# Score matmuls on 32 rows per head, and three phases that hold three sequences in flight

## The chip, the cores and the metric

The kernel runs on one core of a Trainium2 chip. The metric is the device time of one execution in microseconds, as the median of the runs. Names: TensorE (PE) multiplies matrices and loads weights (PEld), VectorE (DVE), ScalarE (ACT) and GpSimd (POOL) work on rows, SyncE (SP) issues most DMAs. SBUF is the on-chip memory, PSUM the eight banks that TensorE writes to.

## What is computed

Eight sequences (NB) of 512 rows (T) and 128 columns go through a layer norm, then three additions to the input: causal linear attention of 16 heads of 8 columns, sliding-window attention (64 rows back) and a gated FFN of 512 hidden columns with four layers. A second layer norm follows, then causal softmax attention and a mixture of 8 experts, of which each row takes 2.

```python
xn = layernorm(x)
h = rmsnorm(xn) * norm_w
q, k, v = h @ Wq, h @ Wk, h @ Wv
lin = causal(q_phi @ k_phi.T) @ v / sum          # q_phi, k_phi: 1, x, x*x/2 of q@Wqf, k@Wkf
win = softmax(window(q @ k.T) / sqrt(8)) @ v
x = x + xn + concat(lin, win) @ Wout + ffn(xn)   # silu(xn@w1)*(xn@w2) -> gelu(@h1) -> gelu(@h2) -> @w3
xn = layernorm(x)
x = x + softmax(causal(q2 @ k2.T) / sqrt(8)) @ v2 @ Wo + experts(xn)
```

## The kernel before

**Scores.** A head has 8 columns. For float32 accuracy q and k are split in a high and a low half, and a head has 32 rows (`ROWS`): three rows of 8 for halves, 8 for ones and for the row maximum that is subtracted. Four heads (`HG`) stand in the 128 rows of `Q1`, `QM`, `Q2` [128, G, 512]. The keys `K1`, `K2` are [128, 16, 512]: a head has 32 rows of its own and zeros in the other 96. So each score matmul takes all 128 rows, with the four heads' queries in them, and the zeros drop three of them (lines 515 to 580, the matmul is L549 in `scores_into`).

**Units and banks.** Work of TensorE is cut into units, each into one of 7 PSUM banks in turn. `UNITS` gives the order for each part of the program; each engine follows it by semaphores (`full` and `taken` of a bank). Units of a sequence: `lin` 40 (linear scores, keys times `QM`, ACT squares them), `cmax` 40 and `smax` 32 (scores with rows as output, of which DVE takes the maximum, L1279), `causal` 40 and `slide` 32 (ACT takes the exponential, L920), then projections, transposes (L528), FFN units (`gate`, `up`, `h1`, `h2`, `third_layer`), `mixed_first`, `mixed_causal`. In `lin`, `cmax` and `causal` five units are one pair of heads.

**After a pair** POOL masks it (`mask_tri`, `mask_slide`; L1079, L1082, L1092), DVE too for `slide` (`mask_middle`). After two pairs PE does `weigh` (L606), 32 matmul instructions of probabilities with V into the bank `heads`, four heads side by side in 32 columns of the array each; DVE or ACT copies the heads out, PE turns them (`rows`), DVE divides, PE turns back (`cols`). `probs` has four slots of a pair each; the FFN's hidden layers and the halves of q2 and k2 lie in the same memory, and the maxima's masked copies lie in `hT`, `xnT`, `hrow` and `spare`.

**Row maxima** go from `mx_c`/`mx_s` through a transpose (`turn_max`, L621), DVE's `negate_max` (L1304) and four DMAs of SP (`place_max`, L427) into a row of `Q2`/`Q1`, before `causal` or `slide` scores can start. **Halves** go through HBM: `split_and_send` (ACT makes the high half, DVE the low one, SP sends three times 256 KB), then `fetch` (four DMAs of 192 KB for keys, one of 1 MB for queries).

**Order.** One turn of the loop (line 1643 and its like) has four stages. *Linear*: `lin` of this sequence with `cmax` of the previous one, after `prefix` and the routing of rows. *Causal*: `causal` of the previous sequence with `smax` of this one. *Slide*: `slide` of this one, q, k and the gate/up layers of the next one. *Dense*: `h1`, `h2`, `third_layer` of the next one with `mix_first`, the second norm, q2, k2, v2 and `logits` of this one. An opening part does slide and dense for sequence 0, a tail part `cmax` and `causal` for sequence 7. Then 78 expert tiles follow (L845 to L861).

## Time and profile before

| what | value |
|---|---|
| median of 3 runs | 1597.93 us (1590.97 to 1603.12) |
| profiled execution | 1584.48 us |
| its span, first to last instruction | 1582.7 us |
| mean granted TensorE clock over the span | 0.917 |
| instructions | 28933 |

The profile is of one execution. Busy times of an engine are a union over its instructions, so that overlapping matmuls count once. A mean duration of a matmul holds its latency, and matmuls in a row start earlier than the one before ends. PEclk is the granted share of 2.4 GHz: 1.00 is 2.4, 0.50 is 1.2 GHz.

### The profile page before, as it was taken

Reading aid. Unit: us, or ns where it says so; the run is one execution under the profiler, and the core shown is the slowest. Engines: PE = TensorE matmul, PEld = TensorE weight load, DVE = VectorE, ACT = ScalarE, POOL = GpSimd, SP = SyncE. Lnnn points to the kernel's source line nnn. Section 1 sums busy time; section 2 is a strip of 40 time slices with the busy share of each in tenths; the row PEclk is TensorE's granted clock in tenths of the full one; section 3 lists DMA queues with packets and bytes.
Section 4 is the critical chain, followed back from the end, with each engine's and each line's share of the span. In section 5 each row is a group of like instructions: output and inputs, shape, how many; then the busy total and the mean of one; then the engine's idle time right before and its main releaser. Section 6 shows DMA issues by size and latency. Waiting matters only on the chain.

```text
span 1582.7 us, 28933 instructions
## 1 busy us (share of the span) xinstructions
PE 1363.4 (86%) x9122; PEld 933.8 (59%) x9122; DVE 823.8 (52%) x3372; ACT 708.2 (45%) x1503; POOL 601.5 (38%) x791
## 2 busy tenths in 40 slices
PE   5979878998899789988998899988997885679997
PEld 2555546655565556555656465556555664449997
DVE  3063375436653566347634764366536644826653
ACT  2345236523662356235643364236623640237765
POOL 6123233323341433233413342223414342618787
PEclk9989999997999899989998899979999995679999
DMA  9204400332022302240034004310233004204443
GB/s 264 60 2 113 108 16 7 96 86 62 7 75 65 104 9 68 54 119 10 30 93 114 14 4 120 84 40 7 75 87 82 7 8 149 85 18 62 62 63 48
DMA packets 82248, 102.09 MB, mean 65 GB/s; under 512 B 12473, under 2 KB 43105, under 8 KB 82017
## 3 DMA queue, kind: packets, MB, share of 16 engines
q1 hardware_dynamic: 63616, 86.53, 19.8%
q0 software_dynamic: 14304, 10.61, 4.3%
q10 hardware_dynamic: 4176, 3.01, 0.7%
q8 instruction: 85, 1.39, 0.4%
q14 instruction: 67, 0.54, 0.1%
HBM read 55.44 MB, written 46.37 MB: 64 GB/s over the span
## 4 chain that ended last, share of the span: by engine, by line
PE 62%; DVE 14%; issue 12%; ACT 5%; DMA 3%; POOL 2%; SPq 2%; DVEq 0%; POOLq 0%; ACTq 0%
PE bank L543 14%; PE bank L549 14%; PE heads L606 13%; PE bank L532 6%; PE bank L528 3%; PE bank L853 3%; PE bank L861 3%; DVE xnT_s L1279 2%; ACT probs L920 2%; DVE hrow L1279 2%; PE bank L647 2%; DVE hT_s L1279 2%; DVE mx_c L1279 1%; PE bank L537 1%; SPq L427 1%
## 5 line engine op out<-in xcount | busy, mean ns | idle before, releaser
L920 ACT ACTIVATE probs<-bank 128x512 f32<-128x512 f32 (+2 forms) x896 | 444.6, 578 | 489.4 <-PE bank L549 487.4
L549 PE MATMUL bank<-K,Q 128*128 128x192 f32 (+4 forms) x1024 | 243.9, 335 | 48.0 <-DVE attn L1320 13.7
L1079 POOL TENSOR_SCALAR_AFFINE_SELECT probs<-probs 128x384 f32<-128x384 f32 x256 | 127.7, 521 | 390.3 <-ACT probs L920 356.2
L606 PE MATMUL heads<-probs,V 128*9 128x192 f32 (+4 forms) x3072 | 225.4, 441 | 19.9 <-issue 14.3
L549 PE MATMUL bank<-Q,K 128*128 128x192 f32 (+4 forms) x1024 | 220.4, 329 | 25.3 <-DMA Q<-mrow_s 11.2
L549 PEld LDWEIGHTS bank<-K,Q 128*128 128x128 f32 x1024 | 181.5, 209 | 93.9 <-issue 30.6
L549 PEld LDWEIGHTS bank<-Q,K 128*128 128x128 f32 x1024 | 156.2, 201 | 59.0 <-issue 25.1
L549 PE MATMUL bank<-QM,K 128*128 128x512 f32 (+3 forms) x512 | 145.0, 379 | 44.7 <-DVE gatesT_s L1257 14.2
L606 PEld LDWEIGHTS heads<-probs,V 128*9 128x9 f32 x3072 | 81.0, 97 | 152.9 <-issue 120.0
L1141 POOL DMA_INDIRECT out<-h1T_s x78 | 124.0, 1589 | 54.0 <-ACT h1T_s L1033 27.6
L910 ACT ACTIVATE probs<-bank,sh_s 128x512 f32<-128x512 f32 x64 | 44.0, 687 | 207.9 <-PE bank L543 207.9
L549 PEld LDWEIGHTS bank<-QM,K 128*128 128x128 f32 x512 | 93.7, 219 | 67.1 <-DVE mx_c L1279 18.6
L543 PE MATMUL bank<-probs,h2T_s 128*128 128x512 f32 x256 | 114.2, 595 | 3.6 <-ACT probs L910 3.6
L1025 ACT ACTIVATE h2T_s<-bank,h1T_s 128x128 f32<-128x128 f32 x312 | 88.9, 368 | 62.7 <-PE bank L853 62.7
L543 PE MATMUL bank<-probs,h1T_s 128*128 128x512 f32 x256 | 115.2, 594 | 1.1 <-DVE probs L1447 1.1
L1092 POOL TENSOR_SCALAR_AFFINE_SELECT probs<-probs 128x512 f32<-128x512 f32 x64 | 56.0, 874 | 157.3 <-ACT probs L920 157.1
L1100 POOL TENSOR_TENSOR rs<-pw,half_neg 128x4 f32<-128x4 f32 x32 | 32.3, 1019 | 202.8 <-DVE pw L1241 202.8
L1308 DVE COPY ot<-heads 128x512 f32<-128x512 f32 x64 | 44.1, 690 | 106.0 <-PE heads L606 106.0
L1125 POOL DMA_INDIRECT sorted_rows<-rows,slot_i x64 | 63.4, 991 | 82.5 <-DVE rows L1376 63.9
L853 PE MATMUL bank<-h1T_s,w_in 128*128 128x128 f32 x624 | 84.2, 279 | 0.0
L861 PE MATMUL bank<-w_out,h2T_s 128*128 128x128 f32 x624 | 83.1, 276 | 0.3 <-ACT h2T_s L1025 0.3
L543 PEld LDWEIGHTS bank<-probs,h2T_s 128*128 128x128 f32 x256 | 47.4, 190 | 60.1 <-issue 56.6
(186 smaller groups left out, 2091.6 us busy)
## 6 DMA issues: line engine op xcount, KB each, us to landing
Q<-slots_of_q SPq DMA_DIRECT2D x16, 1024.0 KB, 10.6
K<-slots_of_k SPq DMA_DIRECT2D x64, 192.0 KB
QM<-slots_of_qm SPq DMA_DIRECT2D x8, 1024.0 KB, 8.7
slots_of_q<-Q SPq DMA_DIRECT2D x24, 256.0 KB, 3.0
slots_of_k<-QM SPq DMA_DIRECT2D x24, 256.0 KB, 4.0
slots_of_qm<-Q SPq DMA_DIRECT2D x24, 256.0 KB, 4.1
slots_of_q<-probs SPq DMA_DIRECT2D x24, 256.0 KB, 3.0
slots_of_k<-probs SPq DMA_DIRECT2D x24, 256.0 KB, 3.7
```

The lines of the kernel that those rows point to most:

```text
L532: pe.matmul(to_bank(run, unit)[:, :], w, x, start=True, stop=True).then_inc(full_sem(run, unit), 1)
L543: mm = pe.matmul(to[:, :], w[:, k, c * P:(c + 1) * P], src[k], start=(k == 0), stop=(k == FC - 1))
L549: mm = pe.matmul(to[:, at:at + right.shape[1]], left, right, start=True, stop=True, skip_group_check=True)
L606: mm = pe.matmul(heads[ROWS * i:ROWS * i + D + 1, P * j:P * j + widths[j]], V[:, j, HG * g + i, :], slot_of(kind, 2 * g + i // 2)[:, at:at ...
L853: mm = pe.matmul(tile_hidden_bank(i)[:, c * P:(c + 1) * P], w_in[:, i % WB, c * P:(c + 1) * P], tile_xT[:, i % 2, :], start=True, stop=True)
L861: mm = pe.matmul(tile_out_bank(i), tile_hidden[i % 2][:, c * P:(c + 1) * P], w_out[:, i % WB, c * P:(c + 1) * P], start=c == 0, stop=c == ...
L920: return act.activation(to, bank, func, scale=scale, bias=bias).then_inc(taken_sem(run, unit), 1)
L1025: last = act.activation(tile_hidden[i % 2][:, c * P:(c + 1) * P], tile_hidden_bank(i)[:, c * P:(c + 1) * P], ACT.Gelu, bias=tile_b1[:, i % ...
L1079: pool.affine_select(out=three, in_=three, compare_op=ALU.is_ge, fill=0.0, base=0, pattern=[[0, 3], [1, P]], channel_multiplier=-1)
L1125: pool.indirect_dma_start(out=sorted_rows, out_offset=bass.IndirectOffsetOnAxis(ap=slot_i[:, n:n + 1], axis=0), in_=rows[:, n // K2, n % K ...
L1141: pool.indirect_dma_start(out=out.rearrange("b t d -> (b t) d"), out_offset=bass.IndirectOffsetOnAxis(ap=tile_rows[:, i % XB, P + 1:P + 2] ...
L1279: last = dve.tensor_tensor_reduce(beside[:, at:at + n], bank_of(run, unit)[:, at:at + n], mask, 1.0, NEG, ALU.add, ALU.max, mx[:, to:to + 1])
```

## The change

- **Scores.** `K1` and `K2` become [128, G, 512], without zeros. `of_head` gives a matmul only the 32 rows of its head, of both operands. Pairs of heads are made new (`head_of`): the two heads of a pair have the same 32 rows, and units alternate between two pairs in neighbouring rows, so unit n and unit n + 1 are of different rows. Maxima (`other_rows`) are taken of the two row groups that the scores beside them don't use. The masks of two pairs come due together after ten units (eight for `slide`). The zeroing of the keys is gone.
- **Order.** Three phases take the place of four stages. *Window*: half of `cmax` (20 units) of the previous sequence with all `slide` of this one, then the norm, q, k, gate/up, `v1`, `h1_0` to `h1_2` of the next, `mixed_first`, second norm, q2, k2 of this. *Causal*: 8 `smax` of the next sequence (`WAKE`) with `h1_3` and `logits`, then `causal` of the previous with the other `smax`, `prefix` and the routing of this. *Linear*: `lin` of the next sequence, with `h2`, `third_layer`, the rest of `causal`'s heads, `v2`, and in its second half the first 20 `cmax` of this (`EARLY`). Opening, first, last and tail are the same three phases with parts left out.
- **Buffers.** `hidden` (two sets of four FFN layers), `halves` (six of 512 columns) and `masked` (seven) are buffers of their own; `dens`/`rdens` are one for each group.
- **Weights.** `wout` and `wo1` are loaded in the new order of heads, by 16 DMAs of ACT instead of two.

The core of the diff (what is the same thing again on another engine is left out):

```diff
-LEAD, BEHIND = 12, 8
+PAIRS, TRI, WINDOW = H // 2, 40, 32
+GROUP, WGROUP = TRI // G, WINDOW // G
+def head_of(pair, half):
+    return 8 * (pair // 4) + 4 * half + pair % 4
+def tri_of(n):
+    return 2 * (n // GROUP) + n % 2, n % GROUP // 2
+def other_rows(n, group):
+    return (n // group ^ 1) * group + n % group
+EARLY = 20
+WAKE = 8
+def slide_by(n):
+    return min(WINDOW, 4 * (n + 1 - EARLY))
+WINDOW_WEIGH, WINDOW_TURN = {24: 0, 26: 1, 28: 2, 30: 3}, {26: 0, 28: 1, 30: 2, 32: 3}
+GATE = {27: 0, 28: 1, 29: 2, 30: 3}
+HIDDEN1 = {31: 0, 34: 1, 36: 2}
+CAUSAL_WEIGH, CAUSAL_TURN = {16: 0, 26: 1, 36: 2}, {22: 0, 32: 1}
+LIN_WEIGH, LIN_TURN = {16: 0, 26: 1, 36: 2}, {22: 0, 32: 1}
+HIDDEN2 = {0: 0, 6: 1, 12: 2, 19: 3}
...
-            Q1, QM, K1 = sb("Q1", [P, G, T], F32R, early), sb("QM", [P, G, T], F32R, early), sb("K1", [P, H, T], F32R, early)
+            Q1, QM, K1 = (sb(n, [P, G, T], F32R, early) for n in ("Q1", "QM", "K1"))
+            hidden = sb("hidden", [P, 2, FC, T], F32, early)
+            halves = sb("halves", [P, 6, T], F32R, early)
...
             def body(run, before, this, after):
                 part, b = run
-                if before and this:
-                    place_max(run, "causal_max", mrow_c, Q2, "placed_c")
-                if this:
-                    place_max(run, "slide_max", mrow_s, Q1, "placed_s")
                 if after:
                     for name in ("q1", "k1", "qm1"):
                         split_and_send(run, (b, 1), name)
...
+                    for name in ("k1", "q1", "qm1"):
+                        fetch_sent((b, 1), name)
+                if this:
+                    for name in ("q2", "k2"):
+                        split_and_send(run, (b, 0), name)
+                if before:
+                    place_max(run, "causal_max", mrow_c, Q2, "placed_c")
+                if after:
+                    place_max(run, "slide_max", mrow_s, Q1, "placed_s")
+                if this:
+                    if before:
+                        sp.wait_ge(taken_sem(run, CAUSAL_UNITS[-1]), taken_at(run, CAUSAL_UNITS[-1]))
+                        sp.sem_inc(S["unread"], 1)
+                    for name in ("k2", "q2"):
+                        fetch_sent((b, 0), name)
+                if before:
                     store(run, b - 1)
...
-            def q_part(buf, h, a, n):
-                return buf[:, h // HG, a:a + n]
+            def of_head(buf, h, a, n):
+                i = h % HG
+                return buf[ROWS * i:ROWS * (i + 1), h // HG, a:a + n]
...
+            def window_phase(run, before, this, after):
+                _, b = run
+                now, nxt = (b, 0), (b, 1)
+                if this:
+                    turn_heads(run, now, LIN, 2)
+                    pe.wait_ge(S["placed_s"], due("placed_s", now, PLACED))
+                s = 0
+                for n in range(EARLY, TRI):
                     if before:
                         causal_max(run, n)
+                    while this and s < slide_by(n):
+                        slide_scores(run, s)
                         s += 1
...
+            def causal_phase(run, before, this, after):
...
+                for n in range(WAKE):
+                    if after:
+                        slide_max(run, n)
+                    if n == 1 and before:
+                        turn_max(run, "causal_max", mx_c, CMAX_UNITS[-1])
+                    if n == 2 and this:
+                        wait_taken(run, "xnT2")
+                        project_rows(run, "logits", xnT, wgT[:, :], E)
+                    if n == 3 and after:
+                        dense(run, "h1_3", h1T, hidden_a, 3)
+                if before:
+                    pe.wait_ge(S["placed_c"], due("placed_c", previous, PLACED))
...
+            def linear_phase(run, before, this, after):
...
+                if after:
+                    pe.wait_ge(S["slots_qm1"], due("slots_qm1", nxt, 16))
+                for n in range(TRI):
+                    if after:
+                        tri_scores(run, LIN_UNITS, K1, QM, n)
+                    if n == TRI - EARLY and this:
+                        pe.wait_ge(S["slots_k2"], due("slots_k2", now, PLACED))
+                        pe.wait_ge(S["slots_q2"], due("slots_q2", now, 16))
+                    if n >= TRI - EARLY and this:
+                        causal_max(run, n - TRI + EARLY)
...
+            for g in range(G):
+                for half in range(2):
+                    row, first = ROWS * g + 2 * D * half, D * head_of(2 * g, half)
+                    act.dma_start(wout[row:row + 2 * D, :, :], dram["wout"].rearrange("a p n -> p a n")[first:first + 2 * D]).then_inc(S["mix_weights"], 16)
+                    act.dma_start(wo1[row:row + 2 * D, :], dram["wo1"][first:first + 2 * D, :]).then_inc(S["mix_weights"], 16)
...
-            pool.memset(K1[:, H // 2:H, :].bitcast(F32), 0.0).then_inc(S["keys1_cleared"], 1)
```

## Rows read from the trace of the kernel before

**Rows 1.** The page, part 1: busy us, share, instructions

```profile
PE 1363.4 (86%) x9122; PEld 933.8 (59%) x9122; DVE 823.8 (52%) x3372; ACT 708.2 (45%) x1503; POOL 601.5 (38%) x791
```

**Rows 2.** Windows: length, busy of PE, PEld, DVE, ACT, POOL, PEclk, DMA share, GB/s

```profile
17.00:67.30 50.30, 46.05 (x135) 22.49 (x133) 7.38 (x15) 14.55 (x19) 20.12 (x32) 1.00 0.56 155
67.30:187.10 119.80, 103.75 (x671) 68.09 (x670) 50.80 (x217) 52.46 (x99) 32.01 (x47) 0.91 0.18 52
187.10:1191.70 1004.60, 894.08 (x5854) 577.29 (x5852) 543.08 (x2280) 452.38 (x839) 331.56 (x494) 0.93 0.22 60
1191.70:1327.00 135.30, 107.74 (x831) 75.29 (x831) 76.84 (x349) 58.15 (x116) 46.84 (x79) 0.87 0.11 30
1327.00:1413.00 86.00, 57.45 (x307) 38.46 (x307) 43.96 (x180) 21.30 (x41) 40.67 (x52) 0.71 0.33 98
```

**Rows 3.** The same for the four stages of one turn, and their sum

```profile
519.80:577.50 57.70, 44.41 (x257) 28.65 (x258) 37.02 (x178) 21.73 (x39) 20.27 (x32) 0.85 0.21 56
577.50:612.00 34.50, 30.07 (x271) 21.45 (x269) 23.29 (x140) 24.32 (x46) 13.94 (x28) 1.00 0.02 5
612.00:644.80 32.80, 31.55 (x259) 21.02 (x260) 16.62 (x31) 19.25 (x41) 12.49 (x18) 0.95 0.29 89
644.80:687.30 42.50, 41.56 (x193) 23.62 (x192) 13.17 (x35) 9.62 (x15) 8.04 (x6) 1.00 0.32 84
sum 167.50, PE 147.60 PEld 94.74 DVE 90.10 ACT 74.91 POOL 54.75; mean PE 36.90 PEld 23.69 DVE 22.52 ACT 18.73 POOL 13.69
```

**Rows 4.** Chain of waits, 500 to 720 us: start, us, what

```profile
586.49 3.79 PE bank L549 x25
590.27 0.45 PE bank L528 x4
...
600.59 2.27 PE heads L606 x32
...
624.20 6.89 PE bank L532 x16
...
632.37 0.41 PE bank L628 x2
...
644.86 3.48 PE bank L543 x8
...
652.21 1.31 PE heads L606 x32
...
666.40 1.78 PE bank L638 x16
...
676.50 1.98 PE bank L532 x4
...
683.60 3.69 PE bank L647 x32
```

**Rows 5.** Row maxima by window (L1279), and the page's group of ScalarE

```profile
577.50:612.00 34.50, 15.44 (x108) 1.00 0.02 5
...
sum 167.50, DVE 45.21; mean DVE 11.30
...
L920 ACT ACTIVATE probs<-bank 128x512 f32<-128x512 f32 (+2 forms) x896 | 444.6, 578 | 489.4 <-PE bank L549 487.4
```

**Rows 6.** Busy time by window, where TensorE does maxima alone

```profile
1359.00:1365.60 6.60, 6.60 (x16) 4.07 (x16) 6.60 (x33) 0.00 (x0) 5.08 (x6) 0.50 0.19 62
```

**Rows 7.** Groups of TensorE by shape: xcount, busy us, mean ns

```profile
L606 PE MATMUL heads<-probs,V 128*9 128x512 f32 x512 | 79.0, 694 | 5.3 <-POOL probs L1082 5.2
```

**Rows 8.** Chain of waits: placing the maxima, and keys in the tail

```profile
606.95 0.29 DVE mrow_s L1304
...
612.00 0.92 PE bank L549 x6
...
1330.79 6.39 DMA K<-slots_of_k
```

**Rows 9.** Timeline of ScalarE's queue, one of 21 loads

```profile
12.31 0.60 ACTq L1044 DMA_DIRECT2D b_s<-in_b  x1
```

## What I expect of the change, and why

> **What bounds the kernel now.** I read the page's shares first. No engine is full: TensorE is busy 86% of the span, VectorE 52%, ScalarE 45%, GpSimd 38% [rows 1]. Next, the span cut by sequence: set-up, an opening, the first sequence, six turns of the loop in 1004.6 us (167.4 each), the last, a tail, and 169.7 us of expert tiles after 1413 [rows 2]. The loop is two thirds of the time, so one turn matters most. Cut into its four stages [rows 3] it shows four limits. The dense stage (42.5 us) is matmul: TensorE 41.56 busy, ScalarE 9.62, VectorE 13.17. The linear stage (57.7 us) is nobody's: TensorE 44.41 at a mean clock of 0.85, VectorE 37.02. PE and DVE take turns, each running dry while the other has a block. Causal (34.5) is mixed, slide (32.8) is TensorE again.
>
> I then priced TensorE's work by the chain of waits, at full clock [rows 4]: a score matmul 3.79 / 25 = 0.152 us; a `weigh` block of LIN or CAUSAL 2.27, of SLIDE 1.31; four transposes 0.45; a 512-column projection 6.89 / 8 = 0.86; one hidden unit of the FFN 3.48; `mix_first` 1.78; `v` or `logits`, as wide as a projection or the same number of instructions, 0.85; a pair of `mix_causal` or `prefix` instructions 0.41; `third_layer` 3.69. A sequence has 320 score matmuls.
>
> **The change, part by part.** Nothing of the arithmetic goes away; three things change.
>
> *(1) Order.* The four stages become three phases, each with dense work between scores. TensorE's work at today's prices:
>
> - Window: 32 + 64 score matmuls 14.6; `weigh` 2.27 + 4 x 1.31 = 7.5; 12 turns 5.4; 13 projections 11.2; `v1` 0.85; three hidden units 10.4; `mix_first` 1.8. Sum 51.8.
> - Causal: 128 scores 19.5; 3 `weigh` 6.8; 2 turns 0.9; two `turn_max` 0.7 (an estimate, under two sets of four transposes, 0.9); `prefix` 5 x 0.41 = 2.0; `logits` 0.85; one hidden unit 3.5. Sum 34.3.
> - Linear: 96 scores 14.6; 4 `weigh` 9.1; 6 turns 2.7; `v2` 0.85; `mix_causal` 8 x 0.41 = 3.3; four hidden units 13.9; `third_layer` 3.7. Sum 48.1.
>
> Together 134.2 of 167.4 us. VectorE's 90.1 us [rows 3] split so: the maxima are 45.2 in all [rows 5]. The second row there is 108 records, four to a `slide_max` unit, so 27 units at 0.57; that leaves 26.5 for 40 causal maxima, 0.66 each. Window gets 20 causal maxima (13.2) and most of the copies, splits and gates, about 37; Causal 32 slide maxima (18.3) and the routing, about 28; Linear 13.2 and about 12 more, 25. The split of the rest is my estimate. ScalarE makes a probability unit in 444.6 / 896 = 0.50 us [rows 5]: 40 in Causal 20 us, 40 in Linear 20 us, 32 shorter ones in Window. It is nowhere the largest. GpSimd has 54.75 us a turn [rows 3]; by my count of masks, powers and row DMAs no phase gets over about 23. So Window and Linear are TensorE's, Causal is between VectorE and TensorE.
>
> *(2) Scores on 32 rows, neighbours in other rows.* Today K is 128 rows with zeros for the other heads, so matmuls follow one another. Afterwards unit n and n+1 use different row groups and banks. Before has no row-tiled matmul. The nearest row is `weigh`, whose four column tiles do run at once: 512 instructions of 694 ns mean are a union of 79.0 us, 154 ns each [rows 7]. Bounds: nothing saved (0.152 stays), or all four at once (a quarter, 48.6 to 12.2 us a sequence). Both parts of a unit use the same rows and bank and must follow one another; only the next unit can start beside the second part. I take a half: minus 7.3, 9.7, 7.3 us.
>
> *(3) Changes of array shape.* Scores on 32-row tiles alternate with 128x128 and with the 32-column `weigh`. Today only the 12 `weigh` blocks change the shape, 24 changes; I count 93 after (39, 20, 34). Price: a hidden unit is 3.48 for 8 instructions of 512 columns, 0.435 each; a LIN `weigh` is 8 steps side by side with 2 x 1280 columns, 2.18; it takes 2.27 [rows 4]. So a change costs up to 0.1 us; nothing excludes 0 below, and above, its whole latency, about the 0.3 us by which a 694 ns `weigh` matmul outlasts its column time [rows 7]. I take 0.1: plus 2.9, 1.4, 2.6. The Trainium skill, TensorEngine Tiling (Array Packing), Key Properties, says that changing the tiling mode drains the engine. That speaks against this change; it gives no price, and by the rows the drain is small.
>
> TensorE afterwards: 47.4, 26.0, 43.4.
>
> *Waits.* Window: from `mix_first` done (666.40 + 1.78 = 668.18) to the q2 projection (676.50) is 8.3 us of VectorE, GpSimd and ScalarE [rows 4]. Covered today by h2 units; afterwards by `h1_2` 3.5, four maxima units and two turns, some 5.6, so 2.7 shows. The phase begins on masks of the last linear pair, `up3` must be gated before `h1_0`, rows before cols: 1 to 2 us each. Total 54. Causal: VectorE 28, plus starving while `weigh` holds TensorE. The causal stage takes 10 us over its busiest of VectorE and ScalarE (34.5 against 24.3) [rows 3]; with the 8 maxima and `h1_3` ahead of it I take 8: 36. Linear: 43.4, and its second half (one linear and one maxima unit per step, VectorE-paced) some 5.6: 49. A turn is 139 us.
>
> *DMA.* Today the row maxima are placed with TensorE idle: 606.95 to 612.00 for the window, 5 us a turn; in the tail the fetch of the keys, 6.39 us, has nothing beside it [rows 8]. Afterwards slide maxima are placed at the end of Causal and read after Linear (hidden by 49 us; uncovered 5). `placed_c` is covered by 8 slide maxima and `h1_3`, about 6 us, but its four DMAs stand on SP behind six sends of q2/k2, so it may show 2. k2/q2 are fetched from Causal's last unit on and wanted at Linear's step 20, some 25 us later, against 6.39 for keys and the like for Q [rows 8]: hidden. SP holds that fetch for `CAUSAL_UNITS[-1]` and the store behind it; nobody waits for the store soon.
>
> *Start.* `wout` and `wo1` become 16 DMAs on ScalarE's queue instead of two. One issue is 0.6 to 2 us there [rows 9]; 14 more at about 0.65 make ScalarE's first `hT1` 9 us late, and TensorE with it. The zeroing of K1 and K2 by GpSimd and VectorE goes; it lay in the set-up and beside the opening, where TensorE waits for inputs or has its own 46 us [rows 2], so I take 0 (at most some us of the first fetch).
>
> *Buffers* for FFN, halves and masked copies only take waits off: no price of their own. Table loads on ScalarE go from four to five a sequence (the h2 gelus move into Linear), 1.3 us off the path.
>
> **Sum.** Loop: 6 x (167.4 - 139) = 170. Ends [rows 2], from the same prices: opening 50.3 to 87 (9 late start, then 25, 20, 33 with nothing beside them); first 119.8 to 114; last 135.3 to 93; tail 86.0 to 58. That is 391.4 to 352, 39 less. Expert tiles: unchanged. The profiled execution spans 1582.7 (1584.5 in all); minus 170 minus 39 gives 1374, 1376 in all. The median of the runs stands 13.4 above that execution: forecast **1388**.
>
> **Rivals.**
> - *A: tiles don't run side by side* (the change doesn't do what it says). Scores stay at 0.152: Window and Linear 7.3 more, Causal 8. A turn 161.6, time 1388 + 136 + 18 at the ends = 1542. For it: two parts of a unit share rows. Against: `weigh` overlaps [rows 7].
> - *B: more than a half overlaps.* At a third, 2.5 us less in Window and Linear each: 1388 - 30 - 5 = 1353. The Trainium skill, TensorE: Matmul & The Clock Gate, Part 3, measured 3.07x for four row tiles; it would bring about this time. No row-tiled matmul is in this trace.
> - *C: handoffs.* PE, DVE, ACT and POOL are more tightly chained (slots, masks, heads in pairs). The linear stage shows the price: 57.7 against VectorE's 37, 20 us. With 20 more a turn: 1388 + 120 + 20 = 1528. Against: dense work is always ready in two phases.
> - *D: the clock, the other side.* Where TensorE does only maxima at VectorE's pace, the granted clock is 0.50 (1.2 GHz) though it is busy throughout [rows 6]; the dense stage has 1.00. Side-by-side 32-row matmuls leave more idle time between units. At 1.2 GHz in Causal and Linear: 26 + 43 us more, about 1388 + 414 = 1802. It decides from a share f of TensorE's work at half clock with 117 (1 + f) + 22 = 167.4 + 6.5, f = 0.30. Today about a tenth is. Against: dense blocks stand in every few steps.
> - *A and C together*: about 1600, no change.
>
> **Chances.** Forecast 0.43, A 0.15, B 0.12, C 0.15, D 0.10, A with C 0.05. Range from B to A with some room, 1320 to 1560, which leaves 0.15 to 0.2 out. The likeliest case's own: 1340 to 1440. About 1% is what a measurement here can tell from no change: faster 0.85, same 0.05, slower 0.10.
>
> **What would show it.** A turn of about 139 us in Window 54, Causal 36, Linear 49; score matmuls of neighbouring units starting a few ns apart, and the score line's busy time near half (A: unchanged); `Q<-mrow_s` gone from what TensorE waits for; ScalarE's first table load 9 us later; granted clock at 0.9 or above (D: below 0.8). A turn over 155 with TensorE idle between blocks would be C. I am wrong if a change of shape costs 0.3 us (19 us a turn more), or if sends and fetches reach past their cover.

## The result, and the profile after

The changed kernel takes **1747.82 us** (median of 4 runs, 1740.83 to 1749.87) where the kernel before takes 1600.53 on the same chip (4 runs, 1590.97 to 1603.32): a ratio of **1.092**, 95% interval 1.087 to 1.098. It is 9% slower. Forecast was 1388. The profiled execution spans 1747.6 us, against 1582.7 before.

The page after, part 1 and the clock's row of part 2 (40 slices, tenths of full speed), to be read against [rows 1]:

```profile
PE 1455.8 (83%) x9122; PEld 871.8 (50%) x9122; DVE 813.3 (47%) x3389; ACT 701.1 (40%) x1508; POOL 585.4 (33%) x791
...
PEclk9899779787977888687868796879677656568999
```

The same 9122 matmuls keep TensorE busy 92 us longer, though the scores were to cost half. VectorE, ScalarE and GpSimd do what they did. The second row is the reason: sixes, sevens and eights all along the loop.

Windows by part, columns as in [rows 2]: opening, first sequence, six turns, last sequence with tail, expert tiles. The parts are cut where `third_layer` or `mix_causal` ends.

```profile
17.00:109.80 92.80, 73.96 (x316) 40.63 (x316) 28.94 (x165) 29.52 (x49) 21.84 (x48) 0.91 0.33 86
109.80:238.00 128.20, 110.07 (x700) 63.19 (x699) 61.56 (x261) 50.49 (x98) 40.53 (x55) 0.85 0.27 73
238.00:1340.10 1102.10, 957.10 (x5849) 523.44 (x5849) 532.39 (x2275) 447.63 (x840) 324.59 (x493) 0.80 0.20 54
1340.10:1579.70 239.60, 162.21 (x940) 93.98 (x940) 94.41 (x357) 64.25 (x131) 72.49 (x108) 0.59 0.14 41
1579.70:1747.60 167.90, 150.86 (x1327) 149.62 (x1326) 91.82 (x313) 109.25 (x390) 123.00 (x78) 0.96 0.42 59
```

A turn is 1102.1 / 6 = 183.7 us, not 139, at a mean clock of 0.80 where before had 0.93 [rows 2]. Last sequence and tail fell to 0.59.

One turn by phase (Window, Causal, Linear), to be read against the four stages of [rows 3]:

```profile
615.60:690.50 74.90, 61.60 (x394) 33.80 (x390) 40.15 (x134) 26.99 (x53) 19.41 (x27) 0.86 0.27 76
690.50:737.80 47.30, 43.13 (x257) 25.48 (x256) 25.55 (x158) 21.89 (x40) 14.77 (x22) 0.64 0.12 36
737.80:799.90 62.10, 55.34 (x334) 28.26 (x330) 23.06 (x87) 25.77 (x47) 19.94 (x33) 0.83 0.17 42
sum 184.30, PE 160.07 PEld 87.53 DVE 88.76 ACT 74.66 POOL 54.12; mean PE 53.36 PEld 29.18 DVE 29.59 ACT 24.89 POOL 18.04
```

Forecast were 54, 36 and 49 us with TensorE busy 47.4, 26.0 and 43.4. TensorE is busy 160 us of a turn and not 117. Causal runs at 0.64.

The chain of waits over a part of that turn (start, us, what), prices as in [rows 4]:

```profile
639.95 2.54 PE heads L589 x32
...
648.62 1.31 PE heads L589 x32
...
662.40 3.70 PE bank L522 x8
...
670.44 5.26 PE bank L522 x8
...
693.13 5.33 PE bank L522 x8
```

Work that the change didn't touch got dearer. A hidden unit, 3.48 us before [rows 4], costs 3.70 in one place and 5.3 in two others, where the mean clock is 0.69 and 0.68, so that over half of its time passes at 1.2 GHz. A window `weigh` is still 1.31.

The page's groups for the weighing and the scores:

```profile
L589 PE MATMUL heads<-probs,V 128*9 128x192 f32 (+4 forms) x3072 | 298.7, 548 | 30.7 <-POOL probs L1027 12.8
L528 PE MATMUL bank<-K,Q 32*128 32x192 f32 (+4 forms) x1024 | 251.3, 397 | 51.0 <-DVE mx_c L1246 18.6
```

And the timeline of TensorE where Causal begins (start, us, engine, line, operation):

```profile
702.22 0.36 PE L528 MATMUL bank<-K,Q 32*128 32x192 f32 x1
702.29 0.52 PE L528 MATMUL bank<-Q,K 32*128 32x384 f32 x1
702.38 0.41 PE L528 MATMUL bank<-K,Q 32*128 32x192 f32 x1
```

The scores do overlap: three begin within 0.16 us. So the change does what it says, and rival A is out. What grew beside it is what the clock costs.

**A ledger of a turn.** For every kernel below I took the six turns of the loop, laid the trace's record of the granted clock over TensorE's instructions, and halved what was busy at 1.2 GHz: that is the work at full clock. A change of shape is counted where TensorE goes from one to another of dense work, scores and `weigh`. "Clock" is the other half, what 1.2 GHz cost. Busy time and mean clock can be checked in the windows; the time at 1.2 GHz is 2 x (1 - mean clock) of a window.

| kernel (span) | turn | busy | of it at 1.2 GHz | work at full clock | clock | idle | changes of shape |
|---|---|---|---|---|---|---|---|
| before (1582.7) | 166.9 | 148.7 | 21.8 | 137.8 | 10.9 | 18.2 | 24 |
| after (1747.6) | 183.7 | 159.5 | 64.7 | 127.2 | 32.4 | 24.2 | 97 |
| rows128 (1588.3) | 165.4 | 142.3 | 16.3 | 134.2 | 8.2 | 23.1 | 24 |
| rows64 (1708.3) | 178.0 | 153.6 | 42.5 | 132.3 | 21.3 | 24.5 | 95 |
| causal128 (1712.8) | 180.2 | 154.9 | 48.5 | 130.6 | 24.2 | 25.4 | 83 |
| samerows (1794.1) | 191.3 | 176.5 | 68.4 | 142.3 | 34.2 | 14.8 | 95 |
| before32 (1709.0) | 183.0 | 164.0 | 76.0 | 126.0 | 38.0 | 19.0 | 66 |

At full clock the changed kernel has 10.6 us less work a turn than before. It pays 21.5 more for the clock and 6.0 more idle. The number of changes doesn't set the clock's cost: before32 has the fewest changes of the kernels with 32-row scores (66) and pays the most (38.0), rows64 has 95, as samerows, and pays 21.3 against 34.2.

### The profile page after: what moved, and what is told of

It reads as the page before. It is cut to its first block, busy times and chain, and to the rows that moved or that the text cites. A ratio compares the mean times of both kernels' runs of the same rounds, so it can differ in the third digit from the quotient of the medians.

```text
span 1747.6 us, 29054 instructions
## 1 busy us (share of the span) xinstructions
PE 1455.8 (83%) x9122; PEld 871.8 (50%) x9122; DVE 813.3 (47%) x3389; ACT 701.1 (40%) x1508; POOL 585.4 (33%) x791
## 3 DMA queue, kind: packets, MB, share of 16 engines
q1 hardware_dynamic: 63616, 86.53, 18.3%
## 4 chain that ended last, share of the span: by engine, by line
PE 60%; DVE 19%; issue 9%; ACT 3%; POOL 3%; SPq 2%; DMA 1%; another core or an unknown queue 1%; DVEq 0%; POOLq 0%; ACTq 0%
PE heads L589 17%; PE bank L522 13%; PE bank L528 12%; DVE masked L1246 8%; PE bank L507 5%; PE bank L511 4%; PE bank L798 2%; ACT probs L856 2%; PE bank L806 2%; DVE probs L1295 2%; POOL out L1087 1%; DVE ot L1275 1%; PE bank L516 1%; DVE hrow L1215 1%
## 5 line engine op out<-in xcount | busy, mean ns | idle before, releaser
L1246 DVE CUSTOM_DVE_ANT_0 masked<-bank,causal_neg_s 128x384 bf16<-128x384 f32 (+3 forms) x512 | 228.2, 487 | 293.2 <-PE bank L528 288.1
L589 PE MATMUL heads<-probs,V 128*9 128x192 f32 (+4 forms) x3072 | 298.7, 548 | 30.7 <-POOL probs L1027 12.8
L528 PE MATMUL bank<-K,Q 32*128 32x192 f32 (+4 forms) x1024 | 251.3, 397 | 51.0 <-DVE mx_c L1246 18.6
L528 PEld LDWEIGHTS bank<-K,Q 32*128 32x128 f32 x1024 | 165.7, 233 | 145.4 <-issue 63.1
L528 PE MATMUL bank<-Q,K 32*128 32x192 f32 (+4 forms) x1024 | 193.8, 392 | 25.3 <-DMA Q<-mrow_c 10.6
L1246 DVE CUSTOM_DVE_ANT_0 masked<-bank,slide_neg_s 128x192 bf16<-128x192 f32 (+1 forms) x512 | 141.0, 336 | 103.6 <-PE bank L528 99.6
L528 PEld LDWEIGHTS bank<-Q,K 32*128 32x128 f32 x1024 | 137.5, 233 | 53.4 <-issue 19.9
L522 PE MATMUL bank<-hidden,h1T_s 128*128 128x512 f32 x256 | 135.9, 682 | 9.7 <-DVE hidden L1414 9.7
L528 PE MATMUL bank<-QM,K 32*128 32x256 f32 (+3 forms) x512 | 109.5, 392 | 34.6 <-DVE attn L1287 22.9
L522 PE MATMUL bank<-hidden,h2T_s 128*128 128x512 f32 x256 | 123.2, 626 | 0.1
L507 PE MATMUL bank<-ident_s,ot 128*128 128x128 f32 x384 | 69.6, 309 | 29.9 <-ACT ot L877 19.9
```

The costliest lines, as they stand in the source:

```text
L507: mm = pe.transpose(to[0:rows, t * P:(t + 1) * P], tile(t), ident[:, :])
L522: mm = pe.matmul(to[:, :], w[:, k, c * P:(c + 1) * P], src[k], start=(k == 0), stop=(k == FC - 1))
L528: mm = pe.matmul(to[:, at:at + right.shape[1]], left, right, start=True, stop=True, skip_group_check=True)
L589: mm = pe.matmul(heads[ROWS * i:ROWS * i + D + 1, P * j:P * j + widths[j]], V[:, j, head_of(pair, half), :], slot_of(kind, pair)[:, at:at ...
L1246: last = dve.tensor_tensor_reduce(beside[:, at:at + n], bank_of(run, unit)[:, at:at + n], mask, 1.0, NEG, ALU.add, ALU.max, mx[:, to:to + 1])
```

## The experiments

Ratios are to the kernel before on the same chip; its median was between 1581 and 1601 us on the chips used, so compare ratios and not times.

Theory R: matmuls on 32 rows, standing in a kernel with pauses, make the granted clock fall, and this is the 9%. Theory O: the new order does it, by its handoffs and pauses, whatever the scores' shape. A third, S: the changes of shape cost much more than 0.1 us.

**rows128: the new order, scores on all rows.**

```
-  i = h % HG
-  return buf[ROWS * i:ROWS * (i + 1), h // HG, a:a + n]
+  return buf[:, h // HG, a:a + n]
```

> The kernel after, with score matmuls that read all 128 rows of both operands instead of the head's 32. The scores are then sums over four heads, so the numbers are others; order, buffers, waits and DMAs are those of the kernel after. Theory R (32-row matmuls make the clock fall): granted clock in a turn from 0.80 to about 0.93, a turn from 184 us to about 160, total some 1540 to 1580. Theory O (the new order makes the idle time that lets the clock fall): clock still about 0.80, turn 184 us or more (nothing overlaps), total 1740 to 1800.

Measured: 1590.18 us, ratio 1.005 (1.003 to 1.007). The loop, the last part, and one turn by phase:

```profile
236.70:1229.10 992.40, 853.92 (x5847) 566.70 (x5846) 532.70 (x2275) 450.99 (x840) 323.19 (x492) 0.95 0.22 60
1229.10:1420.40 191.30, 129.52 (x940) 89.72 (x939) 94.99 (x355) 64.15 (x131) 72.72 (x107) 0.82 0.17 52
...
577.37:650.00 72.63, 58.88 (x408) 38.65 (x406) 43.68 (x159) 26.47 (x51) 21.14 (x25) 0.98 0.35 100
650.00:688.50 38.50, 35.92 (x282) 25.35 (x283) 21.42 (x125) 25.79 (x48) 14.55 (x29) 0.96 0.15 28
688.50:741.60 53.10, 45.49 (x283) 28.82 (x281) 23.66 (x96) 22.87 (x41) 18.24 (x30) 0.94 0.10 31
```

The clock is back at 0.95 and nearly the whole 9% with it. Order, buffers and phases together bring nothing, or lose half a percent: theory O falls. Theory R's own sum was a little too good: it had a turn of about 160 us and 1540 to 1580 in all, where 165.4 and 1590 came, since some clock and 23.1 us of idle time stay. A version that computes the scores rightly on 128 rows needs keys with zeros again, 24 KB more per partition for `K1` and for `K2`; by my count of the buffers they don't fit beside the new ones, so it wasn't built.

**before32: the old order, scores on 32 rows**, successive heads in pairs on the same rows.

```
-  return buf[:, h // HG, a:a + n]                      # queries
+  i = h // 2 % HG
+  return buf[ROWS * i:ROWS * (i + 1), h // HG, a:a + n]
...
+  return buf[ROWS * i:ROWS * (i + 1), h, a:a + n]      # keys: k_part, in four places
```

> The kernel before in its own order, with score matmuls on 32 rows (those of the pair, both heads of a pair in the same rows; the second head of a pair reads a zeroed part of the keys, so the numbers are others). Theory R: the clock falls from 0.92 to about 0.80 in the linear and causal stages, total 1680 to 1760. Theory O: clock about 0.92, total 1570 to 1610, or a few us less where neighbours lie in other rows.

Measured: 1714.54 us, ratio 1.085 (1.079 to 1.091). Its loop:

```profile
200.10:1298.00 1097.90, 984.13 (x5845) 579.04 (x5845) 541.61 (x2274) 453.48 (x834) 329.69 (x493) 0.77 0.20 55
```

That is within theory R's range (1680 to 1760). The old order loses the clock too, more than the new one does (0.77). With rows128 this makes a square: 32 rows cost 16.1 us a turn in the old order and 18.3 in the new one.

**samerows: the new order, every score on rows 0 to 31**, so that nothing can run side by side.

```
-  return buf[ROWS * i:ROWS * (i + 1), h // HG, a:a + n]
+  return buf[0:ROWS, h // HG, a:a + n]
```

> The kernel after, with all score matmuls on rows 0 to 31 (the scores of other heads are those of the first head of four, so the numbers are others). Nothing runs side by side, and scores keep TensorE busy for as long as on 128 rows. Theory R: the clock stays at 0.80 or below and the turn gets longer than 184 us, total 1760 to 1850. Theory O, in its form that running side by side makes the idle time: clock up to about 0.9, total 1600 to 1680.

Measured: 1801.32 us, ratio 1.144 (1.136 to 1.152). Its loop:

```profile
247.10:1394.90 1147.80, 1058.85 (x5845) 631.76 (x5845) 533.26 (x2274) 461.58 (x840) 323.46 (x492) 0.81 0.19 52
```

The total is within theory R's range (1760 to 1850) and the clock is that of after (0.80). So overlap neither causes the fall nor prevents it here; it saves 142.3 - 127.2 = 15.1 us of work a turn, of which 9.4 come back as idle time (24.2 against 14.8), so that a turn is 7.6 us shorter. And samerows against rows128, with 71 changes of shape more and no overlap in either, prices those: 8.1 / 71 = 0.11 us each.

**micro_rows: streams of matmuls alone**, 512 columns each.

> A kernel of its own that computes nothing of the reference (its output is a copy of the input): streams of fp32r score-like matmuls, 512 columns, with the granted clock as the thing to read. In order: 140 on 128 rows; 140 on 32 rows, always the same ones; 280 on two row groups in turn; 560 on four in turn; streams on 128 rows between them; 40 pairs of a 128-row and a 32-row matmul; 40 pairs of a 128-row matmul and one of 9 columns; then 56 on 128 rows and 56 on 32 rows, each evacuated by VectorE. Theory R (the clock's gate looks at how much of the array works): 1.00 in the 128-row streams, 0.50 in the stream on the same 32 rows although it has no gap, 0.50 or changing with two groups, 1.00 with four. Theory I (it looks at idle time alone): 1.00 in every stream, 0.50 only where VectorE paces. By either, two groups take half of the time per matmul (107 ns) and four a quarter (53 ns), if all four run at once; a change of shape costs 0.1 us.

Windows (length, busy of PE, PEld, DVE, POOL, clock, DMA share, GB/s): 140 on 128 rows; 140 on 32 rows, always the same; 280 on 32 rows, two groups in turn; 560 on four groups. Then parts of three streams: 128 rows and one of 32 rows in turn, without a pause; 128 rows at VectorE's pace; 32 rows at VectorE's pace.

```profile
12.42:45.91 33.49, 33.49 (x140) 27.31 (x140) 0.00 (x0) 0.00 (x0) 1.00 0.18 51
45.91:102.61 56.70, 56.70 (x141) 43.01 (x140) 0.00 (x0) 0.00 (x0) 0.53 0.00 0
121.17:153.14 31.97, 31.97 (x281) 27.91 (x280) 0.00 (x0) 0.00 (x0) 1.00 0.00 1
169.24:201.21 31.97, 31.97 (x561) 28.38 (x560) 0.00 (x0) 0.00 (x0) 1.00 0.01 3
...
222.00:272.00 50.00, 50.00 (x71) 19.79 (x70) 0.00 (x0) 0.00 (x0) 0.50 0.00 0
354.00:366.00 12.00, 12.00 (x21) 5.74 (x20) 12.00 (x22) 0.00 (x0) 0.50 0.00 1
396.00:420.00 24.00, 24.00 (x41) 11.28 (x40) 24.00 (x42) 0.00 (x0) 0.50 0.00 1
```

One group of 32 rows, without a pause, falls to 1.2 GHz early in its stream and stays there. Two or four groups side by side hold 2.4 GHz, and four bring all of their gain: 57.1 ns a matmul instead of 227, 3.97x. The Trainium skill (TensorE: Matmul & The Clock Gate, Part 3) has 3.07x for four row tiles; this stream does better. Theory I falls on the single group, which has no gap. Theory R missed on two groups, for which it had 0.50 or a changing clock.

The last three rows limit what can be said. 128 rows and a single 32-row matmul strictly in turn ran at 1.2 GHz (0.50), though the trace shows no pause. And 128 rows alone lose the clock too when TensorE starts one only every 0.60 us, at VectorE's pace; 32 rows at that pace do the same. So 32 rows are not the only way to 1.2 GHz.

**micro_shapes: what a change of shape costs.**

> No kernel of the case: streams of matmuls alone, 512 columns each, with 100 matmuls on 128 rows between the streams; the output is a copy of the input. Before it 128 rows and 32 rows in turn took 427 ns from start to start where 128 rows alone took 227, so a change of shape should cost 0.20 us at full clock (twice what I predicted). Streams: I, 64 rows, one half (140): Theory R refined (half of the array at work held 1.00 with two groups of 32): 227 ns, clock 1.00; if the number of rows in one instruction counts, 0.50. J, 64 rows, halves in turn (280): 113 ns, 1.00. K, 20 times 8 of 128 rows and a pair of 32 rows: 2.04 + 2 x 0.2 = 2.45 us a block, L the same with one of 32 rows: the same 2.45, M with a pair of 64 rows: 2.45. N, 20 times 8 of 128 rows and 16 on column tiles: 1.82 + 4 x 0.227 + 0.4 = 3.1. O, 256 on column tiles alone: 57 ns each, and 0.50 if only the working share of the array counts in both directions (9 of 32 columns used), 1.00 if not. P, 40 times 2 of 128 and a pair of 32: 0.454 + 0.227 + 0.4 = 1.08 us. Q, 60 times one of 128 and four of 32: 0.85 us. If changes are free: K 2.04, P 0.68, Q 0.45.

K (8 on 128 rows and a pair on 32), L (8 and one), M (8 and a pair on 64 rows), P (2 on 128 and a pair on 32), Q (one on 128 and four on 32), columns as before:

```profile
146.70:195.80 49.10, 49.10 (x202) 31.96 (x200) 0.00 (x0) 0.00 (x0) 1.00 0.00 0
218.70:267.80 49.10, 49.10 (x182) 31.89 (x180) 0.00 (x0) 0.00 (x0) 1.00 0.00 0
290.70:339.90 49.20, 49.20 (x202) 32.03 (x200) 0.00 (x0) 0.00 (x0) 1.00 0.00 1
...
575.10:618.50 43.40, 43.40 (x161) 19.07 (x159) 0.00 (x0) 0.00 (x0) 1.00 0.00 0
641.00:693.60 52.60, 52.60 (x304) 22.72 (x302) 0.00 (x0) 0.00 (x0) 1.00 0.00 1
```

**micro_pace: the same with pauses.**

> Streams of matmuls alone again, now with pauses: 24 bursts of about 1.8 us of TensorE's work (at full clock), each closed by a 64-column matmul on 128 rows and followed by a wait for a copy on VectorE, first of 64 columns (a pause of some 0.3 us), then of 512 (some 0.8 us). The bursts: 8 matmuls on 128 rows; 16 on 64 rows, halves in turn; 16 on 32 rows, two groups in turn; 8 on 32 rows, one group; 16 on column tiles (32 instructions in the records); 4 on 128 rows and 8 on 32 rows in turn of two groups. Without pauses all but the single 32-row group kept the clock at 1.00. Theory R (what counts is how much of the array works, pauses included): at the short pause 128 rows, 64-row halves and column tiles hold 1.00, pairs of 32 rows fall to 0.50 for part or all of their stream, the single group does so fully; at the long pause more kinds fall, pairs of 32 rows first. Rival P (pauses alone decide, the rows don't matter): at each pause all six kinds show the same clock, 1.00 or 0.50.

Windows with the short pause, 0.29 us after each burst: 128 rows; halves of 64 rows; two groups of 32 rows; one group; column tiles; 128 and 32 rows mixed.

```profile
39.30:95.30 56.00, 49.39 (x209) 37.06 (x207) 4.50 (x23) 0.00 (x0) 1.00 0.00 0
120.70:181.40 60.70, 54.09 (x394) 38.41 (x392) 4.51 (x23) 0.00 (x0) 1.00 0.00 1
206.80:307.90 101.10, 94.49 (x394) 63.40 (x392) 4.50 (x23) 0.00 (x0) 0.51 0.00 0
335.90:436.50 100.60, 93.98 (x209) 62.34 (x208) 4.50 (x23) 0.00 (x0) 0.51 0.00 0
464.90:560.10 95.20, 88.60 (x764) 22.33 (x760) 4.49 (x23) 0.00 (x0) 1.00 0.00 1
585.50:650.80 65.30, 58.70 (x302) 35.31 (x300) 4.49 (x23) 0.00 (x0) 1.00 0.00 1
```

This is the decisive row. Two groups of 32 rows side by side hold 2.4 GHz without a pause and lose it over their whole stream with pauses of 0.29 us. Halves of 64 rows, with as many matmuls, changes of shape and pauses, do not: their period is 2.64 us, that of the 32-row pairs 4.40. At the longer pause (0.52 us measured, not the 0.8 I expected) the picture is the same: pairs and single groups of 32 rows at 0.51, the rest at 1.00; theory R had expected more kinds to fall there. Rival P falls, and theory R holds in what it says of the rows. For pairs of 32 rows it takes the pauses as well; a single group needs none, and 128 rows kept the clock at these pauses but not at VectorE's pace (micro_rows).

**rows64: the new order, scores on 64 rows**, halves for even and odd heads.

```
-  i = h % HG
-  return buf[ROWS * i:ROWS * (i + 1), h // HG, a:a + n]
+  i = 2 * ROWS * (h % 2)
+  return buf[i:i + 2 * ROWS, h // HG, a:a + n]
```

> The kernel after, with every score matmul on 64 rows (heads with even and odd number on different halves of the array) instead of 32; each score then sums two heads, so the output is not the reference's. Numbers of instructions, their order, the changes of shape and what may run side by side are those of the kernel after. Theory R (the granted clock falls because too little of the array works): with twice the rows at work the clock comes back to about that of the 128-row version (0.93) while the overlap stays. A turn had 160.1 us of TensorE work, 66.6 of it at half clock; at full clock but for some 12 us that is 133, plus the 24 idle: 157 us a turn, and 1530 to 1570 in all. Rival S (the changes of shape and the chained handoffs make the 9%, the clock is a by-product): 64 rows change nothing, 1720 to 1750, clock about 0.80.

Measured: 1709.91 us, ratio 1.071 (1.067 to 1.075). Its loop:

```profile
239.80:1308.00 1068.20, 921.36 (x5846) 530.64 (x5846) 533.00 (x2275) 445.85 (x840) 325.41 (x492) 0.86 0.20 56
```

A miss for both: theory R had 1530 to 1570 us and a clock of about 0.93, rival S 1720 to 1750 and 0.80. The clock lies between 32 rows (0.80) and 128 (0.95), and so do time at 1.2 GHz and its price (21.3 us between 32.4 and 8.2). In a stream 64-row pairs held the clock even with pauses; in the kernel they don't fully. A score unit here often stands alone in its half, with maxima and weighing between, and its pauses are of all lengths; which of it decides wasn't separated. The work at full clock is 5.1 us more than in after. There neighbours from different pairs of groups could overlap, which in halves sometimes meet; that is an inference from the order of units, not measured.

**causal128: 128 rows in the Causal phase alone.**

```
+  return buf[:, h // HG, a:a + n]      # all_rows: for slide_max, in place of of_head
...
+  rows_of = all_rows if units is CAUSAL_UNITS else of_head
```

> The kernel after, with the score matmuls of the Causal phase (40 causal units, 32 window maxima) on all 128 rows, those of Window and Linear on 32 as in after. The scores of that phase then sum four heads, so the output is not the reference's. If the cost of 32-row scores lies where they stand: Causal goes from 47.3 to about 39 us a turn, Window (74.9) and Linear (62.1) stay, a turn is 176 and the total about 1675. If the clock of one phase is made by the work before it as well: Window and Linear gain some us too, a turn of 168 to 172, total 1610 to 1645.

Measured: 1715.01 us, ratio 1.075 (1.070 to 1.079). Cut at the first and last score with `QM` and at the transpose of `mx_c`, and averaged over five turns, Causal goes from 46.2 to 39.5 us (rows128: 39.1), Linear from 62.7 to 63.0, Window from 74.9 to 77.7. Causal gains what was expected, so its cost lies where its 32-row scores stand, and the other phases gain nothing from it. But Window gets 2.8 us longer, from a cause that wasn't looked for, and so a turn is 180.2 us and not 176, and the total misses the 1675 of the nearer expectation.

**start: the wait of the keys' fixed rows (with those of masks and routing tables) moved** from before the opening to its first window maximum.

```
+  if n == 0 and run[0] == "opening":
+      pe.wait_ge(S["masks_ready"], 1)
+      pe.wait_ge(S["routing_set"], ROUTING)
+      pe.wait_ge(S["slots_set"], 16 * (len(scratch) + 2 * HG))
...
-  pe.wait_ge(S["masks_ready"], 1)
-  pe.wait_ge(S["routing_set"], ROUTING)
-  pe.wait_ge(S["slots_set"], 16 * (len(scratch) + 2 * HG))
   body(("opening", -1), *PARTS["opening"])
```

> The kernel after, but TensorE waits for the masks, the routing tables and the fixed rows of the keys only before the first slide maximum of the opening, not before the opening's first transpose. In the trace of after TensorE stood 18.0 us for the DMA of the keys' fixed rows there. If that wait is the late start, the first transpose moves from 30.4 to about 17 us and the total falls by 10 to 14 us, to about 1735. Rival (what I predicted: the 16 small loads on ScalarE's queue delay ScalarE): they end at 23.8 us, so only 5 to 7 us come back, about 1741. Third: something later in the opening is the limit (first fetch of q1/k1 behind SP's setup), 0 to 3 us.

The timeline of TensorE in after, its first transpose, with the idle time before it and what ended it:

```profile
30.41 1.09 PE L507 MATMUL bank<-ident_s,hrow 128*128 128x128 f32 x4 [18.02 <-DMA K<-slots_of_k]
```

The same view of start, first transpose and first projection:

```profile
16.88 0.87 PE L507 MATMUL bank<-ident_s,hrow 128*128 128x128 f32 x3 [4.58 <-DMA x<-in_slide_neg]
...
25.59 1.22 PE L511 MATMUL bank<-hT_s,wq_s 128*128 128x512 f32 x1 [6.75 <-ACT hT_s L847]
```

The wait held the first transpose, which moves 13.5 us. Then ScalarE's queue shows, as I had predicted, but only for what was left of it: the projection moves 8.0 (33.6 to 25.6; before has it at 19.9). In all 1741.87 us, ratio 1.089 (1.084 to 1.094), against 1.092 for after: some 5 us, the rival's amount, but the two intervals overlap.

**best128, twice: rows128 with this start and the 16 small loads on GpSimd's queue**, behind its opening.

```
-  act.dma_start(wout[...], ...)      # and wo1, 16 in all
   body(("opening", -1), *PARTS["opening"])      # GpSimd
+  pool.dma_start(wout[...], ...)
```

> What is left when every score is on 128 rows in the new order (sums of four heads, as in the 128-row version of before) and the start is mended twice: TensorE waits for the fixed rows of the keys only at the opening's first slide maximum, and the 16 small loads of wout and wo1 go to GpSimd's queue behind its opening. The 128-row version spanned 1588.3; the first mend moved the first transpose from 30.4 to 16.9 us but the projection only from 33.6 to 25.6, where ScalarE's queue of loads ended at 23.8; before had it at 19.9. If both were all that is late: 8 and 6 us less, about 1574, ratio to before 0.995. If the later parts take it back: 1580 to 1588, ratio 1.000 to 1.005. No mend reaches the end, so a gain over 1% (below 1567) would be a surprise.

Measured: ratio 1.010 (1.005 to 1.016). That misses both expectations (0.995; 1.000 to 1.005) and is more than rows128 had. Here VectorE stood for 9.2 us before the addition of the mixed rows, a pause that rows128 doesn't have (see the pauses below). So both were run again on one chip.

> The 128-row version of before, once more: ratio to before 1.005. If the pauses of VectorE come with the chip or the hour and not with the kernel, they may show here this time, and the total is then some 15 us longer.

> The 128-row version with the mended start, beside the one without it on the same chip. The first projection is 14 us earlier. If nothing later takes that back: 10 to 14 us less than the version beside it, ratio about 0.997. If the last sequence takes it back (as the profile of the first time hinted, 214 us there and not 191): no difference.

rows128b: 1593.77 us, 1.008 (1.005 to 1.011); best128b: 1588.11 us, 1.005 (1.002 to 1.007). The projection starts at 20.0 us, as in before, and the opening ends 5 us earlier (105.5 against 110.7). The whole gains 5.7 us, about half of the 10 to 14 expected if nothing took it back, and no version of the new order beats the kernel before.

**after_again and latepads: where the end lost time besides.** In after's last part VectorE stood, by the view of waits of 1460 to 1495 us (waited for: us in total, times, longest), for something unnamed, while GpSimd issued row transfers:

```profile
DVE y L1408 <- remote: 12.8, 1, 12.8
...
DVE gatesT_s L1224 <- remote: 6.3, 1, 6.3
```

latepads moves the transfers of padding rows behind the tail's masks:

```
-  if this and not after:
-      send_pads()
   ...
   body(("tail", NB), *PARTS["tail"])
+  send_pads()
```

> The kernel after, with GpSimd's 16 transfers of padding rows issued after the tail's masks, not before the tail's maxima. In after VectorE stood 12.8 and 6.3 us before the addition of the mixed rows and the copy of the gates, with no releaser named, while GpSimd issued row transfers back to back. If their issuing holds VectorE up: both pauses go, the 64 maxima of the tail take about 36 us as in the 128-row version and not 49.6, and some 19 us are gained there; the transfers then stand behind the masks of the tail, 16 x 1.27 = 20 us before the expert tiles may start, so the total is within 10 us of after. If they are not the cause, the pauses stay and the total rises by 15 to 20 us.

> The changed kernel itself once more, for the comparison on one chip with the kernel beside it: 1.09 of before; whether VectorE's two pauses are there in this execution is what is looked for.

latepads: 1732.05 us, ratio 1.095 (1.089 to 1.102); after_again: 1728.52 us, 1.096 (1.089 to 1.103). Neither shows a pause of that kind. The last part of the unchanged kernel is now

```profile
1337.80:1550.90 213.10, 150.29 (x940) 89.36 (x940) 94.98 (x358) 64.09 (x131) 72.64 (x108) 0.65 0.16 46
```

26.5 us shorter than in the first profile with the same instructions: TensorE is idle 14.6 us less, and the clock costs 14.2 less. The pauses are 22 us in sum in that view. As after_again is the same kernel, they belong to an execution, not to the change; they aren't the 9% either, since its ratio without them is 1.096. That GpSimd's transfers cause them isn't shown: latepads had nothing to take away, and it is neither faster nor slower than after_again. They came in the profiles of after, start, rows64, causal128 and the first best128, not in those of before, before32, rows128, samerows or the last four.

## Why the prediction was wrong, point by point

The likeliest case, its range and its sign were wrong; the measured time is near rival D (1802), which had a chance of 0.10. The misses sum like this, in us of the profiled execution: six turns 6 x 44.7 = 268, opening 6, first sequence 14, last and tail 89, tiles -2; 1374 + 375 = 1749 (measured 1747.6, the rest is rounding).

- **Base of the turn, right.** TensorE's work of a turn in the new order, unchanged matmuls, came out of the chain prices as 134.2 us [rows 4]. rows128 has 134.2 at full clock. That they agree to the tenth is luck: before, with the same matmuls, has 137.8. The split by phase was poorer: with waits, rows128 has Window at 72.6 us, where 54 + 7.3 - 2.9 = 58 was implied, and Causal at 38.5 where 44 was.
- **Halving of the scores, a term mis-sized.** Credit 24.3 us a turn, half of the scores' 48.6; measured 15.1 (samerows against after). The score line's busy time in the six turns went from 384.8 us to 301.5, part of it at 1.2 GHz, and not to near half. That often a unit has dense work or a transpose beside it and no second score is my reading of the order, not measured.
- **Changes of shape, right in kind and size.** 93 counted, 97 there; 6.9 us net predicted, 8.1 measured (rows128 to samerows), 0.11 each.
- **Idle time, right in sum.** 22.2 us a turn implied (139 - 116.8), 24.2 measured, 23.1 at 128 rows. By phase it is luck: Window 13.3, Causal 4.2, Linear 6.8 in the turn above, where 6.6, 10.0 and 5.6 were implied. Rival C, 20 us more, is out. `Q<-mrow_s` is gone from what TensorE waits for, as predicted; `Q<-mrow_c` shows instead, 10.6 us in all.
- **The clock: the step that failed.** The sum took every price at full clock and had no term for 1.2 GHz, though the turn before already paid 10.9 us for it (mean clock 0.93 [rows 2]). It is 32.4 after. I had put the danger down to idle time between short units, and argued that dense blocks in every few steps keep the clock. The runs show another cause: at the same order and nearly the same idle time (23.1 and 24.2) 128 rows cost 8.2 us of clock and 32 rows 32.4. Rival D had the effect, TensorE's work in Causal and Linear at 1.2 GHz, but its reason was more idle time between units too. That its 1802 lies near is in part luck: it had 69 us a turn more and the ends at full clock, and measured are 44.7 a turn and 107 outside the loop. Its bound for a loss, f = 0.30, wasn't reached (32.4 / 127.2 = 0.25); the kernel lost without it, because the other terms took 12 us more than forecast. Its place was half right: Causal 0.64, Linear 0.83, Window 0.86.
- These four make the turn: 139 + 9.2 + 1.2 + 2.0 + 32.4 = 183.8 us, measured 183.7.
- **Ends.** The opening was forecast as 87 us and takes 92.8; ScalarE's first table load is 13.8 us late (17.83 to 31.60) and not 9, and more than half of that is the wait for the keys' fixed rows, sent on SP's queue, which the change moved ahead of the opening and which I didn't price: without it the projection came 8.0 us earlier (start). Last and tail were to take 151 and take 240. With 128 rows they take 191: 107.7 of work, 61.8 idle, 21.8 clock, where I had let 151 stand for work and waits at full clock. In after the clock costs 68.3 there; after_again, the same kernel, has 213 and not 240. In the tail one sequence alone is in flight and TensorE waits mostly for VectorE and for GpSimd's masks, and [rows 6] had shown 0.50 for just that: it was used for a rival and not for the sum.
- **Order, worth little.** Before against rows128: a turn gives 1.5 us, the last part 33, the opening takes 43, the first sequence 7. That is 1588.3 against 1582.7. Three sequences in flight move idle time about; they don't remove it (18.2 before, 23.1 after).

## What to carry to other kernels

Price TensorE's work at both clocks, and ask of every change that makes matmuls smaller on the array what the granted clock will do: here a saving of 10.6 us of work a turn was turned into a loss of 16.8 by the clock and by idle time. Row groups pay when several groups run side by side in long streams without pauses; scattered in ones and twos through a kernel that waits, they can cost more than they save, and here did. Read a mean clock below 1 in the profile before as a term of the sum, and test a change of shape on the old order first: before32, a dozen changed lines, showed 1.085 of the 1.092.

## What the runs showed of the hardware

- A stream of matmuls on one group of 32 rows, without a pause, was granted 1.2 GHz for nearly all of it (mean 0.53); two groups in turn kept 2.4 GHz without pauses and had 0.51 with pauses of 0.29 us, where 128 rows, 64-row halves, column tiles and a mix kept 1.00.
- 128 rows and a single 32-row matmul in turn, without a pause in the trace, ran at 0.50; one of 128 rows and four of 32 side by side in turn kept 1.00. 128 rows alone, one every 0.60 us, fell to 0.50 as well.
- Going between 128-row and 32- or 64-row matmuls costs 0.20 us at 2.4 GHz (427 ns from start to start, in turn, against 227 for 128 rows alone) and 0.30 at 1.2 GHz (724 against 427); in the kernel 0.11 net.
- Four row groups ran 3.97 times as many matmuls in the same time as 128 rows.
- One and the same kernel showed its last part as 239.6 us and as 213.1, by pauses of VectorE of up to 12.8 us that the trace puts down to nothing. What causes them is open.
